# Loading strips without their first 64 columns and ordering a head's products long and short in turn

## The reference

```
K = 2 * Re(sum_n Ct[h, n] * exp(dtA[h, n] * l))       # one kernel of 512 lags per head
y = irfft(rfft(u, 1024) * rfft(K, 1024))[..., :512]    # causal convolution along l
x = x + (y + u * D) * (l < length[b])                  # first layer, residual
x = x + x @ W.T + bias + (x @ A[id].T) @ B[id].T       # second layer: base product and a rank 16 adapter
```

## Time and profile before

| what | value |
|---|---|
| median of 3 runs | 209.57 us (209.55 to 209.66) |
| the profiled execution | 209.66 us, its span 207.6 us |
| PE busy | 189.7 us, 91% |
| VectorE busy | 168.7 us, 81% |
| ScalarE busy | 121.1 us, 58% |
| moved by DMA | 56.47 MB, mean 272 GB/s |

### The profile page before, as it was taken

How to read it: one execution, slowest core, us unless ns; L and a number is a source line. 1 busy time by engine, 2 the same in 40 slices (tenths; PEclk the granted TensorE clock), 3 DMA queues, 4 the chain that set the end, 5 groups by cost and what they waited for, 6 DMA issues and landing times.

```text
span 207.6 us, 4381 instructions
## 1 busy us (share of the span) xinstructions
PE 189.7 (91%) x1054; PEld 165.7 (80%) x1054; DVE 168.7 (81%) x370; ACT 121.1 (58%) x354; POOL 90.8 (44%) x144
## 2 busy tenths in 40 slices
PE   0049999999999999899999999999999999999993
PEld 0037899999999999788888888888888888888883
DVE  3985698689699997869998788887888878888662
ACT  2798964334546446266775756656666666756530
POOL 4850000002275788078565545446454464544500
PEclk9999999999999999999999999999999999999999
DMA  5984999999999999965876766667666666764334
GB/s 140 384 331 118 348 406 413 407 412 407 409 412 411 407 407 415 379 219 163 288 253 213 240 200 216 204 215 233 202 229 197 223 218 202 227 203 175 102 101 155
DMA packets 21666, 56.47 MB, mean 272 GB/s; under 512 B 3283, under 2 KB 3987, under 8 KB 21395
## 3 DMA queue, kind: packets, MB, share of 16 engines
q1 hardware_dynamic: 18146, 47.55, 61.9%
q0 software_dynamic: 2560, 8.39, 13.3%
q10 hardware_dynamic: 944, 0.36, 0.8%
HBM read 45.64 MB, written 10.65 MB: 271 GB/s over the span
## 4 chain that ended last, share of the span: by engine, by line
PE 81%; DMA 9%; DVE 5%; POOL 1%; issue 1%; SPq 1%; DVEq 0%; ACTq 0%
PE z_ps L945 24%; PE y_ps L983 20%; PE k_ps L983 20%; DMA strip<-k_pad 8%; PE z_ps L971 7%; PE y_ps L1010 2%; PE y_ps L1009 2%; PE k_ps L1010 2%; PE k_ps L1009 2%; DMA par<-params 1%; DMA k_pad<-k_sb 1%; SPq L263 1%; PE y_ps L1032 1%; PE k_ps L1032 1%; PE y_ps L993 1%
## 5 line engine op out<-in xcount | busy, mean ns | idle before, releaser
L945 PE MATMUL z_ps<-xp,strip 128*128 128x512 f32 (+3 forms) x384 | 63.7, 327 | 0.7 <-DMA strip<-k_pad 0.6
L945 PEld LDWEIGHTS z_ps<-xp,strip 128*128 128x128 f32 x384 | 59.3, 197 | 4.9 <-DMA strip<-k_pad 1.1
L417 POOL DMA_INDIRECT b_hl<-b_tab,b_idx x32 | 38.0, 1186 | 16.5 <-issue 8.8
L412 POOL CAST ag<-a_hl 128x128 fp32r x64 | 23.5, 370 | 38.9 <-PE z_ps L971 28.2
L983 PE MATMUL k_ps<-w_hi,xp 128*128 128x512 f32 x120 | 39.5, 390 | 0.0
L983 PE MATMUL y_ps<-w_hi,xp 128*128 128x512 f32 x120 | 39.5, 390 | 0.0
L552 ACT ACTIVATE ag<-a_hl 128x64 fp32r x128 | 25.7, 249 | 21.1 <-issue 20.9
L750 DVE TENSOR_TENSOR xp<-z_all,xp 128x512 fp32r<-128x512 f32 x32 | 27.6, 862 | 5.2 <-ACT xp L462 5.2
L462 ACT ACTIVATE xp<-z_all 128x512 fp32r<-128x512 f32 x32 | 19.8, 627 | 17.1 <-PE z_ps L945 15.6
L983 PEld LDWEIGHTS y_ps<-w_hi,xp 128*128 128x128 f32 x120 | 22.6, 188 | 4.2
L983 PEld LDWEIGHTS k_ps<-w_hi,xp 128*128 128x128 f32 x120 | 22.6, 188 | 4.2
(11 more groups left out here) (139 smaller groups left out, 236.9 us busy)
## 6 DMA issues: line engine op xcount, KB each, us to landing
strip<-k_pad SPq DMA_DIRECT2D x30, 512.0 KB, 8.4
z_all<-x_conv SPq DMA_DIRECT2D x16, 512.0 KB, 8.8
x_t<-x_tile SPq DMA_DIRECT2D x32, 256.0 KB, 2.8
out<-a_raw SPq DMA_DIRECT2D x31, 256.0 KB, 2.5
strip<-k_pad SPq DMA_DIRECT2D x4, 256.0 KB, 3.6
a_raw<-a_t SPq DMA_DIRECT2D x2, 512.0 KB, 8.5
x_t<-b_rows SPq DMA_DIRECT2D x2, 512.0 KB, 9.0
w_sb<-w_t SPq DMA_DIRECT2D x2, 512.0 KB, 9.8
```

The source lines that it names most:

```text
L412: last = g.tensor_copy(ag[:, s, :, :, q, :].rearrange("p c e r -> p e c r"), src)
L417: g.indirect_dma_start(out=b_hl[:, t % BS, :].bitcast(F32), out_offset=None, in_=b_tab, in_offset=bass.IndirectOffsetOnAxis(ap=b_idx[:, t: ...
L945: last = nc.tensor.matmul(z_ps[:, h % ZS, m * P:L], strip[:, h % SS, m * P:(m + 1) * P, t], xp[:, h % XS, 0:LC - m, e, :], start=(n == 0), ...
```

## The change

A strip from the seventh on (head 6 and later) is loaded without its first 64 columns: 3584 bytes a partition in place of 4096. Of that corner of 128 by 64 the upper half (partitions 0 to 63) only ever reads the padding's zeros, which the buffer still holds from its first, whole load. The lower half (partitions 64 to 127) equals columns 64 to 127 of partitions 0 to 63, and ScalarE copies it: `copy_corner(h - 1)` stands behind `split_x(h)` from h = 7 on, waits for strip h - 1 to land, and copies 64 by 128 values. The last copy stands behind the loop. PE waits for the copy as well before it starts a head from the seventh on.

The 12 products of a head are ordered anew: for heads from 2 on the widths run 512, 128, 512, 128, 512, 128, 384, 256, 384, 256, 384, 256; the first two heads run 512 and 384 in turn and then 256 and 128 in turn, with the wait for the second half of the strip in front of the seventh product, as before.

```diff
@@ load_strip @@
-            def load_strip(h, s, j0, j1, done):
-
-                src = bass.AP(tensor=k_pad.tensor, offset=k_pad.offset + 2 * (h * PAD + 1 + j0),
-                              ap=[[2, P], [1, 2 * (j1 - j0)]])
-                sp.dma_start(strip[:, s, j0:j1, :].rearrange("p l e -> p (l e)").bitcast(F32), src).then_inc(done, 16)
+            def load_strip(h, s, j0, j1, done, p0=0):
+
+                src = bass.AP(tensor=k_pad.tensor, offset=k_pad.offset + 2 * (h * PAD + 1 + p0 + j0),
+                              ap=[[2, P - p0], [1, 2 * (j1 - j0)]])
+                sp.dma_start(strip[p0:P, s, j0:j1, :].rearrange("p l e -> p (l e)").bitcast(F32), src
+                             ).then_inc(done, 16)
@@ sync @@
+                elif h < SS:
+                    load_strip(h, h, 0, L, strip_landed[h])
                 else:
-                    load_strip(h, h % SS, 0, L, strip_landed[h % SS])
+                    load_strip(h, h % SS, CORNER, L, strip_landed[h % SS])
@@ scalar @@
+            def copy_corner(h):
+
+                s = h % SS
+                act.wait_ge(strip_landed[s], 16 * (h // SS + 1))
+                act.activation(strip[CORNER:P, s, 0:CORNER, :],
+                               strip[0:CORNER, s, CORNER:2 * CORNER, :].bitcast(F32), ACT.Copy
+                               ).then_inc(corner_copied, 1)
...
                 split_x(h)
+                if h > SS:
+                    copy_corner(h - 1)
                 for k, at in STEPS_AT.items():
                     if h == at[3]:
                         group_sines(k)
...
+            copy_corner(NH - 1)
@@ tensor @@
+            def paired(longer, shorter):
+
+                kinds = ((0, 0), (0, 1), (1, 0))
+                return [(m, t, e) for m0, m1 in zip(longer, shorter) for t, e in kinds for m in (m0, m1)]
+
...
+                if h >= SS:
+                    pe.wait_ge(corner_copied, h + 1 - SS)
...
-                terms = [(m, t, e) for m in range(LC) for t, e in ((0, 0), (0, 1), (1, 0))]
+                terms = paired((0,), (1,)) + paired((2,), (3,)) if h < 2 else paired((0, 1), (3, 2))
...
-                    if h < 2 and (m, t, e) == (LC // 2, 0, 0):
+                    if h < 2 and n == len(terms) // 2:
```

More of the change, by code:

```diff
@@ L23 @@
 PAD = P + L
+CORNER = P // 2
 assert NA * NC == L and 2 * NS == P and 2 * BR == P
@@ L224, in build @@
         first_half = sem("first_half")
+        corner_copied = sem("corner_copied")
         def store_half(engine, n):
```

## The result

The changed kernel takes 211.45 us (median of 4 runs, 210.9 to 211.54) where the kernel before takes 209.61; the ratio is 1.0069, with a 95% interval of 1.0049 to 1.0088. Measured again as the last experiment it was 1.0050 (1.0030 to 1.0071), without one execution of 213.44 us at a mean clock of 0.992, which counts as slow. The change makes it slower by 0.5 to 0.7%, about 1.0 to 1.8 us, and it lies above the forecast range of 208.9 to 210.4.

A forecast was written before the change was run, and what follows sets the result against it. PE, DMA and VectorE were taken as all full during the heads, with no reserve at head 21. Terms -0.28 + 0.38 + 0 = +0.10 us on the 209.57 median gave 209.7, range 208.9 to 210.4.

The forecast's parts named there:

- They move together, so I take 0 with ±0.1: GpSimd's adapter-table remainders start with ScalarE's quarters, move by 0.3 us, and VectorE's remainders beside them move too; 0 ±0.1.
- What bounds: During the heads PE, DMA and VectorE are all full; head 21 has no reserve against VectorE's delay, hidden by PE's busy row.
- Less to load, -0.28: Strips 64 KB shorter land earlier, so PE's 0.3 us stall before head 26 goes; gain 0.28 us.
- The new wait of PE costs nothing: Before heads, strips landing 1.8 to 3.4 us earlier from head 16 on put landing plus 0.34 well ahead; 0.
- First place of the copies, +0.31 at head 21: Iteration 7: copy_corner(6) before ScalarE's table load delays sines, split_x(8) and remainder 8, reaching head 21 as +0.31 us.
- Second place, +0.07: Iterations 18 to 20: copy_corner(17) ends split_x(19) up to 0.1 us later than VectorE wants it; +0.07 at head 21.
- The extra wait, 0.05 hidden: PE's additional wait before a head is one sequencer instruction of 0.05 us, ahead of the array's work.
- copy_corner(31) ... before ScalarE gets there; 0: Behind the heads, the last copy waits for a strip landing at about 78 us, before ScalarE arrives; 0.
- The order, 0 with ±0.01 a head: Reordered head products pay only by hiding weight loads; taken as 0, ±0.01 us a head, ±0.3 us over 32 heads.
- Rival (c): Slower: ScalarE's copies hold back sines and splits more than counted; 210.2, tail to 210.6; measurable past 0.70 at head 21; chance 0.17.

The follow-up runs named there:

- two idle copies: Kernel before plus two ScalarE copies of zeros nobody reads, behind split_x and before the adapter table's quarter at iterations 17 and 18; ratio 1.0033.
- the copies behind: Changed kernel with all 26 copies, each moved to the end of the loop's body, behind the sines and the table's quarter; ratio 1.0153.

## Why the prediction was wrong

The forecast was 209.7 and the measured time 211.45, with 211.0 in the second measurement. The step that failed is the sentence on GpSimd, "They move together, so I take 0 with ±0.1"; a mis-sized copy, a second wait instruction and the stretch behind the heads add to it. Point by point:

- **What bounds.** Right. Head 21 had no reserve, VectorE's chain set it, and a full busy row of PE hid that. PE's wait moved there, as named.
- **Less to load, -0.28.** Right for the strips up to head 26. Strips 16 and 26 took 4.6 and 7.1 us to land (4.7 and 6.5 said), strip 31 took 5.7 in place of the 4.2 said, and no PE time is lost before head 26. In the changed kernel that alone does not show the term: with two idle copies and whole strips, head 21 late by as much, the stall of head 26 is gone too. The kernel with fifteen copies and the old order shows it, which reaches head 21 as early as before and has no stall at 26. "The new wait of PE costs nothing" did not hold before heads 10 and 17 (0.37 and 0.47 us), though head 21 hides both.
- **First place of the copies, +0.31 at head 21.** The delay of the sines was 0.40 and that of remainder 8 0.41, near the forecast of 0.31; that taking it away would bring head 21 forward was wrong, as the kernel with head 6 whole shows: copy_corner(16) then waits for strip 16, and remainder 17 ends when GpSimd lets it.
- **Second place, +0.07.** The size of the copy was wrong. It was put at 0.2 to 0.3 from start to start and took 0.46 of the list, because ScalarE's 512-wide operations overlap their neighbour by 0.1 (0.53 from start to start, 0.63 long) and the copy overlaps on neither side (at iteration 17 it starts 0.65 behind the start of split_x, and the quarter starts 0.34 behind the copy's). Two instructions of line 572 in a row take 0.65 us, so those don't overlap either, but only the duration of one was read from that row.
- **"They move together, so I take 0 with ±0.1".** This step failed, and it is most of the miss at head 21. Quarter, GpSimd and VectorE did not move together: in the seven profiles of the table VectorE's remainder 17 ended 0.54 or 0.55 behind GpSimd's end, wherever it had started between 51.51 and 52.14. GpSimd's first end came 0.58 later: 0.46 by copy_corner(16) in front of the quarter of iteration 17 and 0.25 by split_x(17), which waited for PE, less 0.13 since GpSimd's operation, no longer behind remainder 16, took 1.27 in place of 1.41. copy_corner(17) added 0.46 at the second. At head 21 that is 1.05 us in place of 0.38. Where the 0.25 comes from no run separates; with head 6 whole split_x(17) came 0.44 earlier than in the changed kernel.
- **The extra wait, 0.05 hidden.** It was 0.15 us in the open at head 21, where PE was waiting for VectorE.
- **"copy_corner(31) ... before ScalarE gets there; 0".** Wrong. The strip landed at 80.82, not at 78; ScalarE stood ready 0.19 us before it, its gathers began at 82.30 in place of 79.54, and PE waited 0.4 longer in front of the tiles.
- **The order, 0 with ±0.01 a head.** The 0 was the author's estimate, and no run shows it. What they show: the loads stayed 0.12 apart behind the short products (35.10 and 35.22 in the changed kernel), and a head took 1.93 in place of 1.96, a gain three times the bound. It is worth nothing in the total that could be measured: before head 21 VectorE takes it, and with whole strips the DMA engines (share 1.03).
- **Rival (c)** had the right sign and the right threshold, but its price reached to 210.6 only, with 0.1 for GpSimd and nothing for the stretch behind the heads.

The difference between the two profiles adds up: 1.21 at head 21 (1.05 from VectorE, 0.15 from the sequencer) and 0.4 in the tail are 1.61, less 0.28 at head 26 gives 1.33, beside the 1.3 between the spans. A gain of some 0.3 from the closer heads behind head 21 was taken back, 0.23 of it before head 23, whose remainder (66.81 to 68.55) again ended 0.54 behind a GpSimd operation. The sum is one of two executions; behind the heads the last to come was strip 31 and not head 31, so the parts are not independent. Open is why the unprofiled executions of the changed kernel lie up to 0.6 us above the profiled one at the same clock (210.9 to 211.54).

## What to carry to other kernels

Cost an added instruction by the step from start to start among its neighbours (0.46 us here for a copy of 0.31), and by what stands behind it on its engine: which other engine starts when that is done, and whom that engine holds. A piece of work on an engine with time to spare that fed GpSimd held up VectorE here, although no semaphore joins the two: two idle copies on ScalarE cost 0.7 us. And a copy that replaces part of a load needs a place where the engine is neither about to wait nor behind a wait; fifteen of 26 such places existed here, and taking those alone turned 0.5 to 0.7% slower into 0.2% faster.

## What the runs showed of the hardware

A VectorE remainder (two inputs from SBUF) that starts while a GpSimd operation of two SBUF inputs runs ended 0.54 to 0.56 us behind that operation's end; so it was for remainder 17 in twelve of the fourteen profiles, and alone it takes 0.68. In the thirteenth GpSimd came later (whole strips and copies, above). The fourteenth, with the copies behind, is the other way round: the two start together, the remainder takes its plain 0.68, and GpSimd's operation lasts 1.83 in place of 1.28, until 1.14 behind the remainder's end.

```profile
52.35 1.83 POOL L404 TENSOR_TENSOR a_hl<-a_raw,a_hl 128x512 fp32r<-128x512 f32 x1 [36.62 <-ACT a_hl L555]
...
52.36 0.68 DVE L766 TENSOR_TENSOR xp<-z_all,xp 128x512 fp32r<-128x512 f32 x1
```

The mask operation, which reads one input from PSUM, took 0.68 beside GpSimd all the same: in the kernel before at 56.11, while GpSimd worked from 56.06 to 57.36. For the remainders the table above has 0.54 or 0.55 in every row. What the two engines share, no run here shows.

In the kernel with whole strips and copies the granted clock fell from 1.00 to 0.56 and 0.59 after 2.07 us of idle PE in front of the tiles. Timeline and windows (us, busy PE, PEld, DVE, ACT, POOL, clock, DMA, GB/s):

```profile
88.00 1.85 PE L1016 MATMUL y_ps<-w_hi,xp 128*128 128x512 f32 x4 [2.07 <-DVE xp L896]
...
88.00:90.00 2.00, 2.00 (x5) 1.59 (x6) 1.87 (x6) 0.00 (x0) 0.96 (x1) 0.56 0.26 88
90.00:92.00 2.00, 2.00 (x9) 1.63 (x8) 0.30 (x1) 0.00 (x0) 1.18 (x2) 0.59 0.87 269
92.00:94.00 2.00, 2.00 (x13) 1.75 (x12) 1.35 (x4) 1.22 (x3) 0.77 (x2) 1.00 0.60 219
```

The 0.56 and 0.59 are of the windows from 88 to 92 us; from 92 on it was 1.00 again, as in the changed kernel over all its tiles. The first four products took 1.85 us where they take 1.16 in the changed kernel, and the tiles began 1.5 us more slowly in all (119.5 in place of 118.0 us from the first tile's product to the last). In the kernel with heads 17 to 20 whole an idle stretch of 2.3 us in front of the tiles, in the profiled execution, was followed by clock 1.00 (another of its five executions has a mean clock of 0.992); so the length of the idle stretch alone does not decide it. With the copies behind, four of the five executions have a mean clock of 0.992 and are 1.6 to 2.1 us longer than the fifth, at 0.999.
